# Two tiles of 25 taken from on-chip feature columns instead of gathered, in a graph layer

## The chip, the cores and the metric

One core of one Trainium2 chip. The time is that of one execution on the device, in microseconds, given as the median of several runs.

## What is computed

A layer of a graph network on N = 12500 nodes with 128 features and E = 400000 edges, sorted by destination. `h` is the normalised x, cut at zero. Each edge makes a message from the features of its two ends and 32 attributes of its own, the messages of a node are added up, and a gated unit makes the new features.

```python
h = jnp.maximum(_layernorm(x, axis=-1), 0.0)
hh = jnp.concatenate([h[src], h[dst], edge_attr_32], axis=-1)
m = jax.nn.relu(hh @ w1 + b1) @ w2 + b2
agg = jax.ops.segment_sum(m, dst, num_segments=12500)
gi = agg @ w_ih + b_ih
gh = h @ w_hh + b_hh
r = jax.nn.sigmoid(i_r + h_r)
z = jax.nn.sigmoid(i_z + h_z)
n = jnp.tanh(i_n + r * h_n)
return x + (1.0 - z) * n + z * h
```

## The kernel before, in words

A first stage (to about 85 us) normalises x, keeps `hT`, the features of all nodes as columns (128 partitions x 12544), in on-chip memory, and stores `p_rows`, the product of each node's features with the first third of w1, to DRAM.

The second stage goes over the edges in 125 chunks, each of five groups, each of five tiles of 128 edges. `step(c, s)` of every engine handles group s of chunk c; the order on each engine is written out by hand, with a lag of one to three steps between engines (`before`, `after`), and semaphores join them. Chunks 0 to 3 and the last are written out; the others are a hardware loop (`over_chunks`). Per group:

- GpSimd gathers the product rows of the edges' sources from `p_rows` into `rows`, one indirect DMA per tile (L488), as soon as the group's buffer is free (`seg_ready`).
- SyncE loads indices (L361), destinations (L378) and edge attributes (L381).
- VectorE makes the comparison table `lhs` (`build_lhs`, L902), adds the gathered rows to TensorE's product (`add_pre`, L934), and makes the table of ones that sorts messages to nodes (`build_onehot`, L893). `add_segments` (L937 to L946) adds the sums of a set of groups to `acc`; `candidate_pre`, `update` and `residual` (L952 to L972) finish the nodes of an earlier chunk. A set is groups 0 to 2 or 3 and 4.
- TensorE multiplies attributes, destination part and bias (`pre_activation`, L1174), sums the messages (`segment_sums`, L1194) and makes the gates (L1208 to L1212).
- ScalarE applies the relu (`relu_message`, L660), copies windows (L634, L640) and applies the gate functions.

One tile of the 25, the last of group 3, is not gathered. Its 128 source columns are copied one by one out of `hT` into `picked`, 96 by ScalarE and 32 by VectorE, 24 and 8 in each of steps 0 to 3, and TensorE multiplies them (L1179). Each engine first loads the node numbers of a step into registers (`load_picks`, L645 on ScalarE, L916 on VectorE), and each copy (L654, L925) then takes its column's address from a register:

```python
for e, node in enumerate(nodes, N_DVE + sum(PICKS_ACT[:s])):
    last = nc.scalar.copy(picked[:, e:e + 1], hT[:, bass.ds(node, 1)])
```

So GpSimd makes 24 gathers in a chunk. The node numbers come with two small loads of SyncE ahead of chunk 0 (L409).

Of the kernel before, what the change touches and what calls it, by code (L numbers as in the profile page):

```python
# [5 lines left out]
ALU = mybir.AluOpType  # L6
ACT = mybir.ActivationFunctionType
AX = mybir.AxisListType
F32 = mybir.dt.float32
I32 = mybir.dt.int32  # L10

P = 128
# [3 lines left out]
N = 12500  # L16
NT = -(-N // P)
NPAD = NT * P
# [12 lines left out]
T = 5  # L31
# [27 lines left out]
PGAP = P + 4  # L59
PICKED = 3  # L60
PICKS_DVE = (8, 8, 8, 8, 0)
PICKS_ACT = (24, 24, 24, 24, 0)
N_DVE, N_ACT = sum(PICKS_DVE), sum(PICKS_ACT)
assert N_DVE + N_ACT == P
IN_RANGE = "src holds node indices, 0 to N - 1"
BASE_IN_RANGE = "the window's base is a least node index, and a minimum holds it at BMAX"
# [6 lines left out]
def gather_tiles(s):  # L73
    return T - 1 if s == PICKED else T


def gnn_kernel(nc, x, src_cols, dst_cols, dst_rows, src_tiles, dst_tiles, ea_t, w1, b1, w2, b2, w_ih, b_ih, w_hh, b_hh, out):
# [3 lines left out]

    q_rows = nc.dram_tensor("q_rows", [NPAD, D], F32, kind="Internal").ap()
    sum_rows = nc.dram_tensor("sum_rows", [NPAD, ROW], F32, kind="Internal").ap()

    with ExitStack() as ctx:
        def sb(name, shape, dt=F32):
            return ctx.enter_context(nc.sbuf_tensor(name, shape, dt))
# [31 lines left out]

        base_i = low[ED:ED + 1, at:at + CHUNKS * NSETS].bitcast(I32)  # L120
        at += CHUNKS * NSETS
        assert at <= NPAD

        pick_dve = low[2 * ED:2 * ED + 1, 0:CHUNKS * N_DVE].bitcast(I32)
        pick_act = low[3 * ED:3 * ED + 1, 0:CHUNKS * N_ACT].bitcast(I32)
# [4 lines left out]
        onehot = sb("onehot", [P, 1 + max(ONEHOT_PLACE), T, WB])  # L130
        base_bc = sb("base_bc", [P, CHUNKS * NSETS])
        lhs = sb("lhs", [P, G, T, PGAP])
# [6 lines left out]
        w1_keep = sb("w1_keep", [P, D])  # L139
        picked = sb("picked", [P, P])  # L140
        idx = sb("idx", [P, G, T], I32)
# [98 lines left out]
        fin_chain = sem("fin_chain")  # L240
        pick_in, picked_dve, picked_act = (sem(n) for n in ("pick_in", "picked_dve", "picked_act"))

        g_zeroed, g_mask_set, g_scattered, g_chain, g_b1_in = (sem(n) for n in ("g_zeroed", "g_mask_set", "g_scattered", "g_chain", "g_b1_in"))
# [66 lines left out]
        def _(sp):  # L310
# [30 lines left out]
            sp.dma_start(dst_nat, dst_rows).then_inc(dstn_in, 16)  # L341
            sp.dma_start(w1_keep[:], w1[0:D, :]).then_inc(weights_in, 16)
            turns = BATCHES // 2 - LOADS_AHEAD
            with sp.Fori(0, turns - 1) as i:
# [49 lines left out]
            def fast():  # L394
                load_destinations(0)
                for s in range(AHEAD):
                    load_group(0, s)

                sp.wait_ge(acc_zeroed, 2)
                for par in range(2):  # L400
                    sp.wait_ge(p_stored[par], BATCHES // 2 * 16)
                    sp.wait_ge(hT_kept[par], BATCHES // 2)
                sp.dma_start(deg[0:1, 0:N], acc[0:1, 0:N]).then_inc(deg_zeroed, 16)
                sp.wait_ge(ranges_ready, 1)
                sp.wait_ge(w2ih_copied, 2)
                tile = PICKED * T + T - 1
                nodes = src_tiles.rearrange("(c k) p -> k c p", k=G * T)[tile:tile + 1, :, :]
                for row, first, last in ((pick_dve, 0, N_DVE), (pick_act, N_DVE, P)):
                    sp.dma_start(row.rearrange("o (c e) -> o c e", e=last - first), nodes[:, :, first:last]).then_inc(pick_in, 16)  # L409
                over_chunks(sp, chunk)  # L410
# [121 lines left out]
        def _(act):  # L532
# [109 lines left out]
            def load_picks(c, s):  # L642
                if isinstance(c, int) and c == 0:
                    act.wait_ge(pick_in, 32)
                _, nodes = nc.values_load_multi_w_load_instructions(  # L645
                    pick_act[0:1, bass.ds(c * N_ACT + sum(PICKS_ACT[:s]), PICKS_ACT[s])], (mybir.EngineType.Activation,),
                    min_val=0, max_val=N - 1, skip_runtime_bounds_check_because=IN_RANGE)
                return nodes

            def pick_columns(c, s, nodes):  # L650

                wait(act, pre_ready[PICKED], c)
                for e, node in enumerate(nodes, N_DVE + sum(PICKS_ACT[:s])):
                    last = nc.scalar.copy(picked[:, e:e + 1], hT[:, bass.ds(node, 1)])  # L654
                last.then_inc(picked_act, 1)

            def relu_message(c, s):
                act.wait_ge(summed[s], c + 1)
                m = rows[:, s, 0:gather_tiles(s), :]
                nc.scalar.activation(m, m, ACT.Relu).then_inc(message_ready[s], 1)  # L660
                if s == PICKED:

                    nc.scalar.activation(rows[:, s, T - 1, :], pre_ps[s % 2][:, (T - 1) * D:GE], ACT.Relu).then_inc(message_ready[s], 1)
# [22 lines left out]
            def step(c, s):  # L686
# [11 lines left out]
                if old:  # L698
                    relu_message(*old)
                if exists((c, s)) and PICKS_ACT[s]:  # L700
                    pick_columns(c, s, load_picks(c, s))
                if s == 0 and ending is not None:
# [68 lines left out]
        def _(dve):  # L771
# [141 lines left out]
            def load_picks(c, s):  # L913
                if isinstance(c, int) and c == 0:
                    dve.wait_ge(pick_in, 32)
                _, nodes = nc.values_load_multi_w_load_instructions(  # L916
                    pick_dve[0:1, bass.ds(c * N_DVE + sum(PICKS_DVE[:s]), PICKS_DVE[s])], (mybir.EngineType.DVE,),
                    min_val=0, max_val=N - 1, skip_runtime_bounds_check_because=IN_RANGE)
                return nodes

            def pick_columns(c, s, nodes):

                wait(dve, pre_ready[PICKED], c)
                for e, node in enumerate(nodes, sum(PICKS_DVE[:s])):
                    last = nc.vector.tensor_copy(picked[:, e:e + 1], hT[:, bass.ds(node, 1)])  # L925
                last.then_inc(picked_dve, 1)

# [46 lines left out]
            def step(c, s):  # L974
# [9 lines left out]
                if exists((c, s)):  # L984
                    build_lhs(c, s)
                    if s in ENDS:
                        sum_counts(c, ENDS[s])
                if s != 1 and old:
                    add_pre(*old)
                if old:  # L990
                    build_onehot(*old)
                if exists((c, s)) and PICKS_DVE[s]:
                    pick_columns(c, s, load_picks(c, s))
                if s == 1 and exists((c, s)):
# [36 lines left out]

            def fast():
                over_chunks(dve, chunk)
# [61 lines left out]
        def _(pe):  # L1095
# [64 lines left out]
            def pre_activation(c, s):  # L1160

                old = before(c, s, {0: 1, 1: 3}.get(s, 2))
                if old and old[1] == PICKED:

                    pe.wait_ge(message_ready[PICKED], old[0] * 2 + 2)
                elif old:
                    pe.wait_ge(summed[old[1]], old[0] + 1)
# [4 lines left out]
                for t in range(T):  # L1172
                    gathered = t < gather_tiles(s)
                    last = nc.tensor.matmul(pre_ps[s % 2][:, t * D:(t + 1) * D], lhs[:, s, t, 0:P],  # L1174
                                            rhs[:, k, :], start=True, stop=gathered)
                    if not gathered:
                        pe.wait_ge(picked_dve, (c + 1) * sum(n > 0 for n in PICKS_DVE))
                        pe.wait_ge(picked_act, (c + 1) * sum(n > 0 for n in PICKS_ACT))
                        last = nc.tensor.matmul(pre_ps[s % 2][:, t * D:(t + 1) * D], picked[:], w1_keep[:], start=False, stop=True)  # L1179
                last.then_inc(pre_ready[s], 1)  # L1180

            def segment_sums(c, s):

                k = SET_OF[s]
                pe.wait_ge(onehot_ready[s], c + 1)
                pe.wait_ge(message_ready[s], c * 2 + 2 if s == PICKED else c + 1)
                old = set_before(c, k)
# [168 lines left out]
```

## Time and profile before

| | us |
|---|---|
| median of 3 runs | 3851.58 |
| lowest, highest | 3850.6, 3860.34 |
| time of the profiled execution | 3857.86 |
| its span | 3856.0 |
| GpSimd, TensorE busy | 2861.7, 2920.9 |
| VectorE, ScalarE busy | 2076.1, 1921.0 |

The span is from the first to the last instruction. Busy time counts what an engine itself executes; register loads, register arithmetic and waits of its sequencer are not in it, and are seen only when a single source line is asked for. PE is TensorE, DVE VectorE, ACT ScalarE, POOL GpSimd, SP SyncE; a q behind the name is the engine's sequencer.

### The profile page before, as it was taken

Reading aid. Unit: us, or ns where it says so; the run is one execution under the profiler, and the core shown is the slowest. Engines: PE = TensorE matmul, PEld = TensorE weight load, DVE = VectorE, ACT = ScalarE, POOL = GpSimd, SP = SyncE. Lnnn points to the kernel's source line nnn. Section 1 sums busy time; section 2 is a strip of 40 time slices with the busy share of each in tenths; the row PEclk is TensorE's granted clock in tenths of the full one; section 3 lists DMA queues with packets and bytes.
Section 4 is the critical chain, followed back from the end, with each engine's and each line's share of the span. In section 5 each row is a group of like instructions: output and inputs, shape, how many; then the busy total and the mean of one; then the engine's idle time right before and its main releaser. Section 6 shows DMA issues by size and latency. Waiting matters only on the chain.

```text
span 3856.0 us, 94141 instructions
## 1 busy us (share of the span) xinstructions
PE 2920.9 (76%) x16157; PEld 2660.2 (69%) x16157; DVE 2076.1 (54%) x8517; ACT 1921.0 (50%) x13700; POOL 2861.7 (74%) x3039
## 2 busy tenths in 40 slices
PE   4677877777777778778777777777787787787777
PEld 4666767667667767667767776677676776677676
DVE  5555555555555555555555555555555555555554
ACT  5544555445554545445554455445554455545553
POOL 4677777777777777777777777777777777777775
PEclk8677677777777776776776677767767767767766
DMA  6444444444444444444444444444444444444443
GB/s 172 118 112 112 111 111 112 111 114 112 111 111 112 111 111 111 111 112 112 111 112 112 112 111 111 111 112 111 111 112 111 114 112 111 112 112 111 111 111 80
DMA packets 439213, 433.42 MB, mean 112 GB/s; under 512 B 180040, under 2 KB 331047, under 8 KB 439057
## 3 DMA queue, kind: packets, MB, share of 16 engines
q0 software_dynamic: 96000, 196.80, 23.5%
q1 hardware_dynamic: 314864, 223.36, 19.7%
q10 hardware_dynamic: 28318, 12.94, 1.2%
q14 instruction: 23, 0.19, 0.0%
q8 instruction: 8, 0.13, 0.0%
HBM read 419.89 MB, written 12.82 MB: 112 GB/s over the span
## 4 chain that ended last, share of the span: by engine, by line
POOL 51%; issue 23%; PE 14%; DMA 3%; ACT 3%; ACTq 2%; DVE 1%; POOLq 1%; DVEq 0%; SPq 0%
POOL rows L488 51%; PE ps L1194 6%; DMA rows<-p_rows,idx 3%; ACT picked L654 2%; ACTq L645 2%; PE ps L1174 2%; PE ps L1209 2%; PE ps L1211 1%; PE ps L1208 1%; DVE rows L934 1%; PE ps L1179 1%; PE ps L1212 1%; POOLq L257 0%; POOLq L285 0%; DVE low L946 0%
## 5 line engine op out<-in xcount | busy, mean ns | idle before, releaser
L488 POOL DMA_INDIRECT rows<-p_rows,idx x3000 | 2831.3, 944 | 938.5 <-issue 897.5
L654 ACT COPY picked<-hT 128x1 f32 x12000 | 1181.4, 187 | 552.9 <-issue 552.9
L1174 PE MATMUL ps<-rhs,lhs 128*128 128x128 f32 x6250 | 1113.4, 342 | 73.5 <-DVE rows L934 68.1
L1194 PE MATMUL ps<-onehot,rows 128*128 128x95 f32 x6250 | 1079.8, 338 | 112.5 <-DVE low L946 112.3
L1194 PEld LDWEIGHTS ps<-onehot,rows 128*128 128x128 f32 x6250 | 1039.0, 255 | 150.8 <-issue 150.8
L934 DVE TENSOR_TENSOR rows<-rows,ps 128x640 f32<-128x640 f32 x625 | 495.6, 793 | 1145.8 <-DMA rows<-p_rows,idx 1138.5
L1174 PEld LDWEIGHTS ps<-rhs,lhs 128*128 128x128 f32 x6250 | 1025.3, 252 | 105.2 <-DVE rows L934 71.5
L660 ACT ACTIVATE rows<-rows 128x640 f32<-128x640 f32 x625 | 447.0, 715 | 1214.0 <-DVE rows L934 1210.6
L902 DVE TENSOR_SCALAR_CACHE_REDUCE lhs<-dst_row,node_at 95x640 f32<-95x640 int32 x625 | 543.2, 869 | 5.3 <-DMA dst_row<-in_dst_rows_dram 5.3
L893 DVE TENSOR_TENSOR onehot<-dst_rel,ps 128x475 f32<-128x475 f32 x625 | 400.9, 642 | 0.0
L925 DVE COPY picked<-hT 128x1 f32 x4000 | 349.9, 146 | 8.0 <-DMA low<-in_src_tiles_dram 7.6
L945 DVE TENSOR_TENSOR acc<-acc,ps 128x95 f32 x250 | 63.5, 254 | 519.9 <-PE ps L1197 449.0
L1179 PE MATMUL ps<-w_keep,picked 128*128 128x128 f32 x250 | 72.6, 381 | 340.0 <-ACT picked L654 340.0
L1179 PEld LDWEIGHTS ps<-w_keep,picked 128*128 128x128 f32 x250 | 47.0, 236 | 361.9 <-issue 361.9
L1216 PE MATMUL ps<-ident,upd 128*100 128x128 f32 x123 | 43.7, 356 | 321.7 <-DVE upd L965 321.7
L1209 PE MATMUL ps<-low,b2ih 1*128 (+1 forms) x738 | 268.4, 464 | 0.0
L1216 PEld LDWEIGHTS ps<-ident,upd 128*100 128x100 f32 x123 | 16.9, 137 | 348.1 <-DVE upd L965 347.5
L1208 PE MATMUL ps<-acc,w2ih 128*128 (+1 forms) x738 | 225.9, 408 | 0.0
L1209 PEld LDWEIGHTS ps<-low,b2ih 1*128 1x128 f32 x738 | 178.4, 299 | 62.8 <-issue 59.6
L1208 PEld LDWEIGHTS ps<-acc,w2ih 128*128 128x128 f32 x738 | 192.2, 318 | 0.0
L1211 PE MATMUL ps<-hT,whh_sb 128*128 (+1 forms) x492 | 181.4, 472 | 0.0
L1158 PE MATMUL ps<-w_dst,h_win 128*95 128x128 f32 x500 | 115.7, 319 | 47.4 <-ACT h_win L634 47.4
(101 smaller groups left out, 1372.0 us busy)
## 6 DMA issues: line engine op xcount, KB each, us to landing
dst_row<-in_dst_rows_dram SPq DMA_DIRECT2D x625, 240.0 KB, 3.8
lhs<-in_ea_t_dram SPq DMA_DIRECT2D x625, 80.0 KB
rows<-p_rows,idx POOLq DMA_INDIRECT x3000
idx<-in_src_cols_dram SPq DMA_DIRECT2D x625, 2.5 KB
p_rows<-low SPq DMA_DIRECT2D x14, 448.0 KB, 3.2
x_fin<-in_x_dram ACTq DMA_DIRECT2D x123, 50.0 KB
out_dram<-out_fin ACTq DMA_DIRECT2D x123, 50.0 KB
acc<-in_x_dram SPq DMA_DIRECT2D x13, 448.0 KB, 4.8
```

The costliest lines, as they stand in the source:

```text
L488: pool.indirect_dma_start(out=rows[:, s, t, :], out_offset=None, in_=p_rows[:, :], in_offset=bass.IndirectOffsetOnAxis(ap=idx[:, s, t:t + ...
L654: last = nc.scalar.copy(picked[:, e:e + 1], hT[:, bass.ds(node, 1)])
L660: nc.scalar.activation(m, m, ACT.Relu).then_inc(message_ready[s], 1)
L893: nc.vector.tensor_tensor(onehot[:, ONEHOT_PLACE[s], :, 0:W], dst_rel[:, s * T:(s + 1) * T].unsqueeze(2).to_broadcast([P, T, W]), iota_ps. ...
L902: nc.vector.tensor_scalar(lhs[0:W, s, :, 0:P], dst_row[0:W, s, :].rearrange("w (t p) -> w t p", t=T), node_at[0:W, bass.ds(c * NSETS + SET ...
L925: last = nc.vector.tensor_copy(picked[:, e:e + 1], hT[:, bass.ds(node, 1)])
L934: nc.vector.tensor_tensor(r, r, pre_ps[s % 2][:, 0:k * D], ALU.add).then_inc(summed[s], 1)
L1174: last = nc.tensor.matmul(pre_ps[s % 2][:, t * D:(t + 1) * D], lhs[:, s, t, 0:P], rhs[:, k, :], start=True, stop=gathered)
L1194: done = nc.tensor.matmul(sg[:, 0:W], rows[:, s, t, :], onehot[:, ONEHOT_PLACE[s], t, 0:W], start=(first and t == 0), stop=(last and t == ...
L1208: nc.tensor.matmul(gate_ps[:, g, :], w2ih[:, cols], a, start=True, stop=False)
L1209: last = nc.tensor.matmul(gate_ps[:, g, :], b2ih[0:1, cols], d, start=False, stop=(g == 2))
L1211: nc.tensor.matmul(gate_ps[:, g, :], whh_sb[:, cols], h, start=False, stop=True)
```

## The change

Two tiles of the 25, the last of groups 3 and 4, are copied from `hT`; GpSimd makes 23 gathers a chunk. The 256 columns are shared as 120 to ScalarE (24 in each of five steps) and 136 to VectorE (32, 24, 24, 24, 32). ScalarE's copies see `picked` and `hT` as bytes and take four bytes from an address that is already in bytes: VectorE makes it once, as node x 4 + 66688, for all chunks, it goes to DRAM (`pick_dram`) and comes back in rows on one partition. VectorE's copies take f32 words by the node number as before. SyncE loads ten rows instead of two, ScalarE's five after the store of the made places. VectorE loads its registers ahead of `add_pre`, and copies the first half of its columns ahead of `build_onehot` and the second half behind it. TensorE waits for the relu of a copied tile only before its last tile.

```diff
-PICKED = 3
-PICKS_DVE = (8, 8, 8, 8, 0)
-PICKS_ACT = (24, 24, 24, 24, 0)
+PICKED = (3, 4)
+ACT_PICKS = ((0, 24), (56, 24), (104, 24), (152, 24), (200, 24))
+DVE_PICKS = ((24, 32), (80, 24), (128, 24), (176, 24), (224, 32))
...
+HT_AT = 66688
...
 def gather_tiles(s):
-    return T - 1 if s == PICKED else T
+    return T - 1 if s in PICKED else T
...
+                sp.wait_ge(places_ready, 1)
+                sp.dma_start(pick_dram, places).then_inc(places_stored, 16)
+                sp.wait_ge(places_stored, 16)
+                for k in range(G):
+                    first, n = ACT_PICKS[k]
+                    sp.dma_start(pick_act[k].rearrange("o (c e) -> o c e", e=n),
+                                 pick_dram.rearrange("(o c) e -> o c e", o=1)[:, :, first:first + n]).then_inc(pick_in, 16)
+                    first, n = DVE_PICKS[k]
+                    tile, e = PICKED[first // P] * T + T - 1, first % P
+                    sp.dma_start(pick_dve[k].rearrange("o (c e) -> o c e", e=n),
+                                 src_tiles.rearrange("(c k) p -> k c p", k=G * T)[tile:tile + 1, :, e:e + n]).then_inc(pick_in, 16)
...
-                for e, node in enumerate(nodes, N_DVE + sum(PICKS_ACT[:s])):
-                    last = nc.scalar.copy(picked[:, e:e + 1], hT[:, bass.ds(node, 1)])
+                for k in part:
+                    e = 4 * (first + k)
+                    last = nc.scalar.copy(picked_bytes[:, e:e + 4], hT_bytes[:, bass.ds(found[k] - HT_AT, 4)])
...
+            dve.wait_ge(src_in, 16)
+            nc.vector.tensor_scalar(places, places, 4, HT_AT, ALU.mult, ALU.add).then_inc(places_ready, 1)
...
+                    found = load_picks(c, s)
+                    half = DVE_PICKS[s][1] // 2
                 if s != 1 and old:
                     add_pre(*old)
+                if exists((c, s)):
+                    pick_columns(c, s, found, range(half))
                 if old:
                     build_onehot(*old)
-                if exists((c, s)) and PICKS_DVE[s]:
-                    pick_columns(c, s, load_picks(c, s))
+                if exists((c, s)):
+                    pick_columns(c, s, found, range(half, len(found)))
...
+                    if t == T - 1 and old and old[1] in PICKED:
+
+                        pe.wait_ge(message_ready[old[1]], old[0] * 2 + 2)
```

How it moves instructions. VectorE, step 3 of the loop's chunk, before (L902 is the comparison, L934 the addition, L893 the onehot, L916 the register load, L925 the copies, each with one register operation, listed as ISA):

```order
L902 TENSOR_SCALAR lhs,count<-dst_row,node_at 95x5x128
L934 TENSOR_TENSOR rows<-rows,ps 128x640 [waits rows_in1,pre_ready1]
L893 TENSOR_TENSOR onehot<-dst_rel,ps 128x5x95 [waits dst_rel_ready,seg_ready4]
L916 ISA
L916 TENSOR_LOAD low
L925 ISA [waits pre_ready3]
L925 COPY picked<-hT 128x1
```

The same step in the changed kernel (L935 is the comparison, L952 the load, L970 the addition, L960 the copies):

```order
L935 TENSOR_SCALAR lhs,count<-dst_row,node_at 95x5x128
L952 ISA [waits pre_ready4]
L952 TENSOR_LOAD low
L970 TENSOR_TENSOR rows<-rows,ps 128x640 [waits rows_in1,pre_ready1]
L960 ISA
L960 COPY picked<-hT 128x1
```

The load stands ahead of the addition; behind the addition come 12 pairs of ISA and COPY, then the onehot (L926), then 12 more pairs. The loop of VectorE has 128 rows before and 336 now.

ScalarE, step 3 of the loop's chunk, before (L660 is the relu, L645 the load, L654 the copies, each of the 24 with an ISA between):

```order
L660 ACTIVATE rows<-rows 128x640 [waits summed1]
L645 ISA
L645 TENSOR_LOAD low
L654 ISA [waits pre_ready3]
L654 COPY picked<-hT 128x1
```

And changed (L691 the relu, L675 the load, L684 the copies):

```order
L691 ACTIVATE rows<-rows 128x640 [waits summed1]
L675 ISA [waits pre_ready4]
L675 TENSOR_LOAD low
L684 COPY picked<-hT 128x4 x24
```

The register operations between the copies are gone, and step 4, which had no copies, has the same rows.

## Rows read from the trace of the kernel before

**Rows 1.** The page, part 1: engine, busy us, share of the span, instructions.

```profile
PE 2920.9 (76%) x16157; PEld 2660.2 (69%) x16157; DVE 2076.1 (54%) x8517; ACT 1921.0 (50%) x13700; POOL 2861.7 (74%) x3039
```

**Rows 2.** Lines of GpSimd, 200 to 3800 us: busy, mean ns, idle before.

```profile
L488 POOL DMA_INDIRECT rows<-p_rows,idx x2884 | 2721.6, 944 | 878.9 <-issue 864.3 <-PE ps L1194 14.6
```

**Rows 3.** Timeline of VectorE over one chunk: start, us, what [idle before].

```profile
2002.91 0.69 DVE L934 TENSOR_TENSOR rows<-rows,ps 128x512 f32<-128x512 f32 x1 [3.15 <-DMA rows<-p_rows,idx]
2003.52 0.64 DVE L893 TENSOR_TENSOR onehot<-dst_rel,ps 128x475 f32<-128x475 f32 x1
...
2008.02 0.25 DVE L945 TENSOR_TENSOR acc<-acc,ps 128x95 f32 x1 [3.18 <-PE ps L1197]
...
2008.79 0.82 DVE L934 TENSOR_TENSOR rows<-rows,ps 128x640 f32<-128x640 f32 x1 [0.36 <-DMA rows<-p_rows,idx]
...
2015.12 0.82 DVE L934 TENSOR_TENSOR rows<-rows,ps 128x640 f32<-128x640 f32 x1 [1.72 <-DMA rows<-p_rows,idx]
...
2018.84 0.88 DVE L902 TENSOR_SCALAR_CACHE_REDUCE lhs<-dst_row,node_at 95x640 f32<-95x640 int32 x1
...
2021.27 0.82 DVE L934 TENSOR_TENSOR rows<-rows,ps 128x640 f32<-128x640 f32 x1 [1.55 <-DMA rows<-p_rows,idx]
...
2027.66 0.82 DVE L934 TENSOR_TENSOR rows<-rows,ps 128x640 f32<-128x640 f32 x1 [2.86 <-DMA rows<-p_rows,idx]
```

**Rows 4.** Source line L925, 2010 to 2012 us: sequencer and engine, first and last start.

```profile
L925 DVEq FUSED_REGOPS  x8: 46/46/46, 2010.1 to 2010.9; - x8
L925 DVE COPY picked<-hT x8: 136/138/143, 2010.9 to 2011.3; 128x1 f32 x8
```

**Rows 5.** Timeline of VectorE in chunk 0.

```profile
108.10 0.95 DVE L925 COPY picked<-hT 128x1 f32 x8
```

**Rows 6.** Register loads by source line: ns min/median/max, first and last start.

```profile
L916 DVEq TENSOR_LOAD <-low x500: 598/620/837, 105.1 to 3819.2; - x167
L645 ACTq TENSOR_LOAD <-low x500: 1475/1661/1695, 105.1 to 3820.0; - x167
L937 DVEq TENSOR_LOAD <-low x250: 318/529/544, 124.9 to 3841.3; - x125
L628 ACTq TENSOR_LOAD <-low x250: 279/457/470, 93.2 to 3806.4; - x125
```

**Rows 7.** Timeline of ScalarE, step 1 of the same chunk.

```profile
2009.65 0.74 ACT L660 ACTIVATE rows<-rows 128x640 f32<-128x640 f32 x1 [0.80 <-DVE rows L934]
2011.53 2.32 ACT L654 COPY picked<-hT 128x1 f32 x24 [1.15 <-issue]
```

**Rows 8.** Busy us (and count) of one chunk: PE, PEld, DVE, ACT, POOL; then TensorE's picks.

```profile
1997.60:2027.50 29.90, 23.84 (x125) 21.57 (x125) 16.19 (x66) 14.94 (x109) 22.59 (x25) 0.68 0.46 112
...
2026.45 0.77 PE L1179 MATMUL ps<-w_keep,picked 128*128 128x128 f32 x2 [2.93 <-ACT picked L654]
```

**Rows 9.** Timeline around chunk 0: SyncE's small loads, the first picks, chunk 1.

```profile
98.17 1.50 SPq L409 DMA_DIRECT2D low<-in_src_tiles_dram  x2
...
106.05 0.85 DVE L925 COPY picked<-hT 128x1 f32 x7 [7.62 <-DMA low<-in_src_tiles_dram]
...
117.09 0.87 DVE L902 TENSOR_SCALAR_CACHE_REDUCE lhs<-dst_row,node_at 95x640 f32<-95x640 int32 x1
```

**Rows 10.** Timeline of VectorE behind the last chunk's steps.

```profile
3830.50 0.69 DVE L934 TENSOR_TENSOR rows<-rows,ps 128x512 f32<-128x512 f32 x1 [3.74 <-DMA rows<-p_rows,idx]
...
3836.71 0.82 DVE L934 TENSOR_TENSOR rows<-rows,ps 128x640 f32<-128x640 f32 x1 [4.96 <-DMA rows<-p_rows,idx]
```

**Rows 11.** DMA issues: KB each, median us from issue to landing.

```profile
base_bc<-base_f_dram ACTq DMA_DIRECT2D x1, 125.0 KB, 3.0
```

**Rows 12.** Timeline of GpSimd while VectorE copies.

```profile
2011.26 0.94 POOL L488 DMA_INDIRECT rows<-p_rows,idx  x1 [0.30 <-PE ps L1194]
```

**Rows 13.** The page, part 3: DMA queues of the instructions: packets, MB.

```profile
q14 instruction: 23, 0.19, 0.0%
q8 instruction: 8, 0.13, 0.0%
```

More of the change, by code:

```diff
@@ L10 @@
 I32 = mybir.dt.int32
+U8 = mybir.dt.uint8
 P = 128
@@ L59, with turns_of @@
 PGAP = P + 4
-PICKED = 3
-PICKS_DVE = (8, 8, 8, 8, 0)
-PICKS_ACT = (24, 24, 24, 24, 0)
-N_DVE, N_ACT = sum(PICKS_DVE), sum(PICKS_ACT)
-assert N_DVE + N_ACT == P
-IN_RANGE = "src holds node indices, 0 to N - 1"
+PICKED = (3, 4)
+ACT_PICKS = ((0, 24), (56, 24), (104, 24), (152, 24), (200, 24))
+DVE_PICKS = ((24, 32), (80, 24), (128, 24), (176, 24), (224, 32))
+assert sorted(e for first, n in ACT_PICKS + DVE_PICKS for e in range(first, first + n)) == list(range(len(PICKED) * P))
+def turns_of(picks, slot):
+    return max(k + 1 for k, (first, _) in enumerate(picks) if first < (slot + 1) * P)
+HT_AT = 66688
+IN_RANGE = "src holds node indices, 0 to N - 1, and they are made into places in a row of hT"
 BASE_IN_RANGE = "the window's base is a least node index, and a minimum holds it at BMAX"
@@ L118, in gnn_kernel, with pick_row @@
         at += 2 * NB * D
[L120 to L125, printed above, removed]
+        base_i = low[ED:ED + 1, NPAD - CHUNKS * NSETS:NPAD].bitcast(I32)
+        assert at <= NPAD - CHUNKS * NSETS
+        def pick_row(part, at, picks):
+            out = []
+            for _, n in picks:
+                out.append(low[part:part + 1, at:at + CHUNKS * n].bitcast(I32))
+                at += CHUNKS * n
+            assert at <= N
+            return out
+        pick_act = pick_row(ED, 0, ACT_PICKS[:4]) + pick_row(2 * ED, 0, ACT_PICKS[4:])
+        pick_dve = pick_row(2 * ED, CHUNKS * ACT_PICKS[4][1], DVE_PICKS[:2]) + pick_row(3 * ED, 0, DVE_PICKS[2:])
         dst_int = sb("dst_int", [P, G * T], I32)
@@ L130, in gnn_kernel @@
         onehot = sb("onehot", [P, 1 + max(ONEHOT_PLACE), T, WB])
+        places = onehot[:, :, :, :].rearrange("p g t w -> p (g t w)")[0:CHUNKS, 0:len(PICKED) * P].bitcast(I32)
         base_bc = sb("base_bc", [P, CHUNKS * NSETS])
@@ L241, in gnn_kernel @@
         pick_in, picked_dve, picked_act = (sem(n) for n in ("pick_in", "picked_dve", "picked_act"))
+        src_in, places_ready, places_stored = (sem(n) for n in ("src_in", "places_ready", "places_stored"))
         g_zeroed, g_mask_set, g_scattered, g_chain, g_b1_in = (sem(n) for n in ("g_zeroed", "g_mask_set", "g_scattered", "g_chain", "g_b1_in"))
@@ L342, in _ @@
             sp.dma_start(w1_keep[:], w1[0:D, :]).then_inc(weights_in, 16)
+            first, gap = PICKED[0] * T + T - 1, (PICKED[1] - PICKED[0]) * T
+            picked_tiles = src_tiles.rearrange("(c k) p -> c k p", k=G * T)[:, first:first + gap + 1:gap, :]
+            sp.dma_start(places.rearrange("c (k p) -> c k p", p=P), picked_tiles).then_inc(src_in, 16)
             turns = BATCHES // 2 - LOADS_AHEAD
@@ L405, in fast @@
                 sp.wait_ge(w2ih_copied, 2)
[L406 to L409, printed above, removed]
+                sp.wait_ge(places_ready, 1)
[9 more added lines that the diff above has]
+                                 src_tiles.rearrange("(c k) p -> k c p", k=G * T)[tile:tile + 1, :, e:e + n]).then_inc(pick_in, 16)
                 over_chunks(sp, chunk)
@@ L642, in load_picks, with pick_columns @@
             def load_picks(c, s):
[L643 to L652, printed above, removed]
-                for e, node in enumerate(nodes, N_DVE + sum(PICKS_ACT[:s])):
-                    last = nc.scalar.copy(picked[:, e:e + 1], hT[:, bass.ds(node, 1)])
-                last.then_inc(picked_act, 1)
+                if isinstance(c, int) and c == 0 and s == 0:
+                    act.wait_ge(pick_in, 32 * G)
+                first, n = ACT_PICKS[s]
+                wait(act, pre_ready[PICKED[first // P]], c)
+                _, found = nc.values_load_multi_w_load_instructions(
+                    pick_act[s][0:1, bass.ds(c * n, n)], (mybir.EngineType.Activation,),
+                    min_val=HT_AT, max_val=HT_AT + 4 * (N - 1), skip_runtime_bounds_check_because=IN_RANGE)
+                return found
+            def pick_columns(c, s, found, part):
+                first = ACT_PICKS[s][0]
+                for k in part:
+                    e = 4 * (first + k)
+                    last = nc.scalar.copy(picked_bytes[:, e:e + 4], hT_bytes[:, bass.ds(found[k] - HT_AT, 4)])
+                if part[-1] == len(found) - 1:
+                    last.then_inc(picked_act, 1)
             def relu_message(c, s):
@@ L699, in step @@
                     relu_message(*old)
-                if exists((c, s)) and PICKS_ACT[s]:
-                    pick_columns(c, s, load_picks(c, s))
+                if exists((c, s)):
+                    pick_columns(c, s, load_picks(c, s), range(ACT_PICKS[s][1]))
                 if s == 0 and ending is not None:
@@ L913, in load_picks, with pick_columns @@
             def load_picks(c, s):
[L914 to L917, printed above, removed]
-                    min_val=0, max_val=N - 1, skip_runtime_bounds_check_because=IN_RANGE)
[L919 to L926, printed above, removed]
+                if isinstance(c, int) and c == 0 and s == 0:
+                    dve.wait_ge(pick_in, 32 * G)
+                first, n = DVE_PICKS[s]
+                wait(dve, pre_ready[PICKED[first // P]], c)
+                _, found = nc.values_load_multi_w_load_instructions(
+                    pick_dve[s][0:1, bass.ds(c * n, n)], (mybir.EngineType.DVE,),
+                    min_val=0, max_val=N - 1, skip_runtime_bounds_check_because=IN_RANGE)
+                return found
+            def pick_columns(c, s, found, part):
+                first = DVE_PICKS[s][0]
+                for k in part:
+                    last = nc.vector.tensor_copy(picked[:, first + k:first + k + 1], hT[:, bass.ds(found[k], 1)])
+                if part[-1] == len(found) - 1:
+                    last.then_inc(picked_dve, 1)
             def add_pre(c, s):
@@ L1162, in pre_activation @@
                 old = before(c, s, {0: 1, 1: 3}.get(s, 2))
-                if old and old[1] == PICKED:
-                    pe.wait_ge(message_ready[PICKED], old[0] * 2 + 2)
-                elif old:
+                if old:
                     pe.wait_ge(summed[old[1]], old[0] + 1)
@@ L1176, in pre_activation @@
                     if not gathered:
-                        pe.wait_ge(picked_dve, (c + 1) * sum(n > 0 for n in PICKS_DVE))
-                        pe.wait_ge(picked_act, (c + 1) * sum(n > 0 for n in PICKS_ACT))
-                        last = nc.tensor.matmul(pre_ps[s % 2][:, t * D:(t + 1) * D], picked[:], w1_keep[:], start=False, stop=True)
+                        slot = PICKED.index(s)
+                        pe.wait_ge(picked_dve, c * G + turns_of(DVE_PICKS, slot))
+                        pe.wait_ge(picked_act, c * G + turns_of(ACT_PICKS, slot))
+                        last = nc.tensor.matmul(pre_ps[s % 2][:, t * D:(t + 1) * D], picked[:, slot * P:(slot + 1) * P], w1_keep[:],
+                                                start=False, stop=True)
                 last.then_inc(pre_ready[s], 1)
@@ L1185, in segment_sums @@
                 pe.wait_ge(onehot_ready[s], c + 1)
-                pe.wait_ge(message_ready[s], c * 2 + 2 if s == PICKED else c + 1)
+                pe.wait_ge(message_ready[s], c * 2 + 2 if s in PICKED else c + 1)
                 old = set_before(c, k)
```

9 lines of the change are left out of this document (6 added, 3 removed).

## The prediction

> **What bounds the kernel now.** I read the page's busy times first, then the grouped lines of GpSimd, then one chunk of VectorE in order of time, and last the single source lines, because only there do the instructions of an engine's sequencer (register loads and register arithmetic) show. The page gives no engine more than 76% [rows 1], so it names no bound. GpSimd does: between 200 and 3800 us its 2884 gathers take 944 ns each, and nearly all its idle time is "issue", 864 us, or 0.30 us per gather; only 14.6 us are waits for TensorE [rows 2]. So the gathers follow each other every 1.249 us, 24 of them make a chunk of 29.95 us, and 125 chunks make the kernel. Everything else waits for them: VectorE's addition stands idle until the rows have come in five of the six places of a chunk where it waits [rows 3].
>
> **What the change removes.** One gather per chunk: 23 x 1.249 = 28.7 us. If GpSimd still bounded, 125 x 1.249 = 156 us would go.
>
> **What it adds on VectorE.** The path that matters there is not the engine's but its sequencer's. In the chunk of rows 3, eight register operations of the picks run from 2010.1 to 2010.9, seven intervals, so 0.114 us each, while the eight copies that they feed, handed over in advance behind a longer operation, start within 2010.9 to 2011.3, 0.06 us apart [rows 4]. So a copied column costs the engine 0.06 us and the sequencer 0.114 us, and when nothing longer is in front the copies come out at the sequencer's pace: eight in 0.95 us, (0.95 - 0.15)/7 = 0.114 [rows 5]. VectorE now copies 136 columns per chunk instead of 32, still with a register operation each: 104 x 0.1145 = **11.9 us** more.
>
> Then the register loads. VectorE's load of eight node numbers takes 0.62 us in the median (0.60 to 0.84), its load of one value 0.53; ScalarE's load of 24 takes 1.66, its load of one 0.46 [rows 6]. From ScalarE a value costs (1.66 - 0.46)/23 = 0.052 us; from VectorE's own pair (0.62 - 0.53)/7 = 0.013, or 0.044 with the slower half of its loads (0.84). I take ScalarE's slope, because its load has the new size: 24 values 1.65 us, 32 values 2.08 us. Three and two of them make 9.1 us per chunk where four loads of eight, 0.6 and 0.82 in turn, made 2.85: **+6.3 us**, and 0.1 for issuing a fifth. With the low slope they would be 3 x 0.83 + 2 x 0.93 = 4.3 us, only 1.5 more; with 0.06 a value they would reach 10.5, 7.7 more. Those are the two ends.
>
> To what does this add? VectorE's sequencer waits only at its six marked places. Each wait is the idle time in brackets in rows 3 and, since the sequencer is through once it has handed out the instruction in front, the part in which that one still runs: 3.15 and 0.8 of a comparison, 4.0; 3.18 less a register load of 0.53, 2.6; 0.36 and 0.2, 0.6; 1.72 and 0.1, 1.8; 2018.84 to 2021.27, 2.4; 2.86 and 0.1, 3.0. That is 14.4, or 14.0 with the hand-over itself taken off, in a turn of 29.95, so its own work is about 16.0 us [rows 3], and the sum **16.0 + 11.9 + 6.3 + 0.1 = 34.3 us**. That is more than GpSimd's 28.7 and more than the 29.95 of now: 14 us of room are filled with 18.3 us of new work. The long operations do not add to it: an addition (0.82), a table of ones (0.64) or a comparison (0.87) runs while the sequencer loads registers or hands out the next twelve copies (1.37 us). The addition of group 4 is shorter by a tile (0.69 against 0.82), which is hidden too.
>
> **What waits for VectorE then.** In a step the register load now stands ahead of the addition, and half of the copies ahead of the onehot, as the rows of the program order show. Where VectorE has time, the load falls into the wait for the rows and costs nothing; in a chunk that VectorE bounds, there is no such wait, and the addition, the relu, the segment sums and the release of the row buffers all come later. GpSimd will then stand at its wait for the segment sums, about 34.3 - 28.7 = 5.6 us a chunk.
>
> **ScalarE.** It copies 120 columns instead of 96 and loses its register operations. Its 24 copies take 2.32 us, 0.093 each, and the idle time before them is 1.15 us of load behind a relu [rows 7]. I cost the removed register operation at nothing, since copies were already at the engine's pace as far as these rows tell (each lasts longer than the 0.093 us between two starts); four bytes instead of a word I cost between 0 and 0.09 us each. A step is 1.88 us from the relu's start to the first copy [rows 7] and 2.3 of copies; five of those, two window copies with their loads (0.9 each) and the gate functions (1.3) make about 24 us, 35 at the high end of the byte copies, where it would only draw level with VectorE. Fifth turn, one relu of a tile more (0.26 us): inside. TensorE has one product pair of picks more a chunk, 0.77 us on 23.8 [rows 8], with 10 us of room in a chunk of 34.3.
>
> **Start and end.** The first picks started at 106.05 us, 7.9 us after SyncE issued their two small loads at 98.17, 0.75 us each [rows 9]. Now SyncE first stores the made places (0.75 to issue, about 3.0 to land, the landing time of a small transfer of ScalarE's in the same phase [rows 11]), waits, and issues ten such loads, 7.5 us; with the same 6.4 us of landing the first copy comes near 98.2 + 3.7 + 7.5 + 6.4 = 115.8, **9.7 us later**. Making the places is one operation on 125 partitions in front of it, hidden in SyncE's earlier work. Chunk 0 had 11.0 us of VectorE from there (106.05 to the first comparison of chunk 1 at 117.09 [rows 9]) and gets 18.3 more: 29.3. Chunks 1 and 2 have no finishing work on VectorE (candidate, update, residual, 1.6 us): 32.7 each. 122 chunks at 34.3 are 4184.6. Behind the last one the old kernel needed 3856.0 - 3826.8 (3830.50 less 3.74 of waiting) = 29 us, with waits for the last gathers of 3.74 and 4.96 us in it [rows 10]; TensorE's work behind them stays, so I take off 5: 24. Sum: 115.8 + 29.3 + 65.4 + 4184.6 + 24 = **4419 us** of span. The profiled execution had a span of 3856.0 and a time of 3857.9, and the median of the three runs is 3851.6, 6.3 below it; so 4419 + 1.9 - 6.3 = 4415 as a median.
>
> Its own range: the period is good to about 1 us (overlap of the chained operations, the load of 32): 4290 to 4540; with the ends of the load cost 3830 and 4590.
>
> **Against a rule.** While VectorE's eight copies ran from 2010.9 to 2011.3 [rows 4], a gather began at 2011.26, 0.30 us behind the one before and 0.94 long, like all the others [rows 12]: copies cost GpSimd nothing. The Trainium skill, SBUF — State Buffer, "Who interferes with whom", says that VectorE copies can take the port pair shared with GpSimd and block its making of descriptors. By that rule 136 copies of 0.06 us could add 8.2 us to GpSimd's 28.7, a chunk of 36.9. The trace speaks against it at this shape.
>
> **Rivals.**
> - *GpSimd stays the bound, 3705 us, 8%.* The sequencer would have to hand out columns at the engine's 0.06 us: 34.3 - 136 x 0.0545 = 26.9, under 28.7. Then 3857.9 - 156 + 9.7 - 6.3 = 3705. For it: the engine can do it [rows 4]; against: the register operations never come closer than 0.114. The decision lies at 5.6 us per chunk, 0.073 us a column.
> - *Long register loads are cheap, about 3840 us, 6%.* With the low slope a chunk is 16.0 + 11.9 + 1.5 + 0.1 = 29.5, and gain and loss cancel: 115.8 + 24.5 + 55.8 + 3599 + 24 = 3819, up to 3840 with 0.2 us more a chunk. Against: ScalarE's 1.66 us.
> - *The longer loop has to be fetched in every turn, about 4780 us, 9%.* VectorE's loop grows from 128 to 336 rows of program. A transfer per turn of 3.0 us [rows 11] on top gives 122 x 3.0 = 366 more. Against: ScalarE's loop of 228 rows ran with 31 packets on the instruction queues in the whole run [rows 13], so it was fetched once. The Trainium skill, Runtime: NRT & Kernel Launch, "Instruction fetch mechanics", says that the buffer holds two blocks of 256 instructions and that a branch out of them stalls; by that rule it hangs on where the 336 lie.
> - *Copies do block GpSimd, about 4740 us, 2%*, with a chunk of 36.9.
> - *ScalarE bounds through slow byte copies, 4300 to 4600 us, 3%*: a slower outcome too, only with another engine in front.
>
> **How the numbers follow.** Forecast 72%; together nine in ten lie above the present time. Range: 4150 to 4800 leaves out the first two rivals (14%) and holds the fetch and port cases and the unknown costs between. A difference under 0.3%, some 12 us, counts as no change, and a measurement of this kernel can tell no less. Faster 0.10 (the first rival and a share of the second), same 0.02, slower 0.88.
>
> **What would show it.** Right: GpSimd's idle before its gathers put down to TensorE's sums, some 5 us a chunk; VectorE's wait for rows gone; VectorE loads of 1.6 and 2.1 us; register operations 0.114 apart; VectorE busy near 16.2 + 104 x 0.06 = 22 us of 34 [rows 8], so never "full" on the page. Wrong: gathers still every 1.25 us without waits (first rival), loads under 1 us (second), thousands of packets on the instruction queues (third), gathers longer than 0.95 us (fourth), or VectorE waiting for ScalarE's picks through TensorE (fifth).

## The result and the profile after

The changed kernel takes 4464.6 us in the median (4462.55 to 4465.33, four runs) against 3852.6 us of the kernel before: a ratio of 1.158, 95% interval 1.157 to 1.160, 612 us slower. The forecast was 4415 (4150 to 4800).

The page of the changed kernel, part 1 (engine, busy us, share of the span, instructions), answers to [rows 1]:

```profile
PE 2838.4 (64%) x16407; PEld 2634.7 (59%) x16407; DVE 3155.7 (71%) x21518; ACT 2212.8 (50%) x16825; POOL 2742.7 (61%) x2914
```

GpSimd fell from 74% to 61% busy; VectorE is the highest now, but at 71% it looks as if it had room. The longest wait of the changed kernel, and the waits of VectorE's addition and of GpSimd (total us, times, longest):

```profile
ACT rows L691 <- DVE rows L970: 1415.0, 621, 7.7
DVE rows L970 <- issue: 846.9, 499, 2.5
POOL rows L515 <- issue: 808.4, 2529, 1.1
POOL rows L515 <- PE ps L1238: 690.6, 201, 23.7
POOL rows L515 <- PE ps L1241: 141.2, 144, 2.3
```

In the kernel before, the same view has this line of VectorE's addition:

```profile
DVE rows L934 <- DMA rows<-p_rows,idx: 1138.5, 533, 5.0
```

Where the addition waited 1138 us for gathered rows, it now waits for no one that the profile shows ("issue"), ScalarE's relu waits 1415 us for the addition, and GpSimd waits 832 us for TensorE's segment sums, some 6.7 us in each of 125 chunks. On GpSimd's timeline this stands as two kinds of row; the gathers themselves are unchanged, 0.94 us with 0.30 between [rows 2, 12]:

```profile
2001.17 0.94 POOL L515 DMA_INDIRECT rows<-p_rows,idx  x1 [5.38 <-PE ps L1238]
2002.42 0.94 POOL L515 DMA_INDIRECT rows<-p_rows,idx  x1 [0.31 <-issue]
```

The period can be read off an operation that each chunk has once, VectorE's last addition of the finishing work (source line, 300 to 3600 us: count, ns, first and last start), in the kernel before and, in the second block, in the changed one:

```profile
L972 DVE TENSOR_TENSOR out_fin<-x_fin,ps x110: 286/287/290, 315.8 to 3581.8; 100x128 f32<-100x128 f32 x110
```

```profile
L1008 DVE TENSOR_TENSOR out_fin<-x_fin,ps x94: 286/289/290, 332.6 to 3566.0; 100x128 f32<-100x128 f32 x94
```

3266.0/109 = 29.96 us and 3233.4/93 = 34.77 us. The timeline of VectorE over two steps of one chunk (step 4, then step 0 of the next) answers to [rows 3]:

```profile
2002.99 0.15 DVE L944 TENSOR_REDUCE set_count<-count 95x1 f32<-95x2 f32 x1
2005.35 0.82 DVE L970 TENSOR_TENSOR rows<-rows,ps 128x640 f32<-128x640 f32 x1 [2.21 <-issue]
2006.09 1.25 DVE L960 COPY picked<-hT 128x1 f32 x16
2007.29 0.65 DVE L926 TENSOR_TENSOR onehot<-dst_rel,ps 128x475 f32<-128x475 f32 x1
2007.86 1.42 DVE L960 COPY picked<-hT 128x1 f32 x16
2009.85 0.88 DVE L935 TENSOR_SCALAR_CACHE_REDUCE lhs<-dst_row,node_at 95x640 f32<-95x640 int32 x1 [0.57 <-issue]
...
2012.42 0.69 DVE L970 TENSOR_TENSOR rows<-rows,ps 128x512 f32<-128x512 f32 x1 [1.69 <-issue]
```

The 2.21 us in front of the addition are the register load of 32 values. The source lines show it and the register operations, which no busy share contains; they answer to [rows 6] and [rows 4] (all loads of the run, then the five of one chunk, then the register operations):

```profile
L952 DVEq TENSOR_LOAD <-low x625: 1597/1827/2356, 108.5 to 4434.9; - x157
...
L952 DVEq TENSOR_LOAD <-low x1: 2111/2111/2111, 2003.1 to 2003.1; - x1
L952 DVEq TENSOR_LOAD <-low x1: 2218/2218/2218, 2010.0 to 2010.0; - x1
L952 DVEq TENSOR_LOAD <-low x1: 1829/1829/1829, 2017.7 to 2017.7; - x1
L952 DVEq TENSOR_LOAD <-low x1: 1608/1608/1608, 2024.7 to 2024.7; - x1
L952 DVEq TENSOR_LOAD <-low x1: 1819/1819/1819, 2031.5 to 2031.5; - x1
...
L960 DVEq FUSED_REGOPS  x17000: 46/46/53, 110.9 to 4441.1; - x198
```

9.6 us a chunk are register loads, in which VectorE's sequencer hands out nothing.

### The profile page after: what moved, and what is told of

Its sections match the earlier page's. It is cut to its first block and busy times, and to the rows that moved or that the text cites. A ratio compares the mean times of both kernels' runs of the same rounds, so it can differ in the third digit from the quotient of the medians.

```text
span 4463.5 us, 112268 instructions
## 1 busy us (share of the span) xinstructions
PE 2838.4 (64%) x16407; PEld 2634.7 (59%) x16407; DVE 3155.7 (71%) x21518; ACT 2212.8 (50%) x16825; POOL 2742.7 (61%) x2914
## 5 line engine op out<-in xcount | busy, mean ns | idle before, releaser
L515 POOL DMA_INDIRECT rows<-p_rows,idx x2875 | 2712.3, 943 | 1651.2 <-issue 808.4
L684 ACT COPY picked<-hT 128x4 uint8 x15000 | 1488.5, 189 | 599.4 <-issue 599.3
L960 DVE COPY picked<-hT 128x1 f32 x17000 | 1460.4, 148 | 101.4 <-issue 101.0
L1216 PE MATMUL ps<-rhs,lhs 128*128 128x128 f32 x6250 | 1192.0, 359 | 64.7 <-DVE rows L970 51.9
L1216 PEld LDWEIGHTS ps<-rhs,lhs 128*128 128x128 f32 x6250 | 1112.3, 270 | 85.8 <-issue 65.6
L691 ACT ACTIVATE rows<-rows 128x640 f32<-128x640 f32 x625 | 433.6, 694 | 1420.5 <-DVE rows L970 1415.0
L970 DVE TENSOR_TENSOR rows<-rows,ps 128x640 f32<-128x640 f32 x625 | 477.4, 764 | 847.7 <-issue 846.9
L935 DVE TENSOR_SCALAR_CACHE_REDUCE lhs<-dst_row,node_at 95x640 f32<-95x640 int32 x625 | 543.4, 869 | 79.2 <-issue 68.2
L926 DVE TENSOR_TENSOR onehot<-dst_rel,ps 128x475 f32<-128x475 f32 x625 | 406.0, 650 | 0.0
L1222 PE MATMUL ps<-w_keep,picked 128*128 128x128 f32 x500 | 129.2, 347 | 288.7 <-ACT picked L684 288.7
L1253 PE MATMUL ps<-low,b2ih 1*128 (+1 forms) x738 | 169.7, 309 | 0.0
L1252 PE MATMUL ps<-acc,w2ih 128*128 (+1 forms) x738 | 145.2, 278 | 0.8
L1253 PEld LDWEIGHTS ps<-low,b2ih 1*128 1x128 f32 x738 | 107.9, 183 | 35.9
L1255 PE MATMUL ps<-hT,whh_sb 128*128 (+1 forms) x492 | 114.4, 314 | 0.0
```

The source lines that it names most:

```text
L515: pool.indirect_dma_start(out=rows[:, s, t, :], out_offset=None, in_=p_rows[:, :], in_offset=bass.IndirectOffsetOnAxis(ap=idx[:, s, t:t + ...
L684: last = nc.scalar.copy(picked_bytes[:, e:e + 4], hT_bytes[:, bass.ds(found[k] - HT_AT, 4)])
L926: nc.vector.tensor_tensor(onehot[:, ONEHOT_PLACE[s], :, 0:W], dst_rel[:, s * T:(s + 1) * T].unsqueeze(2).to_broadcast([P, T, W]), iota_ps. ...
L935: nc.vector.tensor_scalar(lhs[0:W, s, :, 0:P], dst_row[0:W, s, :].rearrange("w (t p) -> w t p", t=T), node_at[0:W, bass.ds(c * NSETS + SET ...
L960: last = nc.vector.tensor_copy(picked[:, first + k:first + k + 1], hT[:, bass.ds(found[k], 1)])
L970: nc.vector.tensor_tensor(r, r, pre_ps[s % 2][:, 0:k * D], ALU.add).then_inc(summed[s], 1)
```

## The experiments

The theory: VectorE's sequencer sets the period, by a sum of copies with register operations, register loads and its old work. The rivals: waits for other engines behind the moved load and the later addition; the engine's own time; the loop being fetched anew. Periods below are from the same once-a-chunk operation as above.

**e1, bytes on both engines.** VectorE copies as ScalarE does, from ready addresses; SyncE loads its rows from `pick_dram` too.

```diff
...
-                    last = nc.vector.tensor_copy(picked[:, first + k:first + k + 1], hT[:, bass.ds(found[k], 1)])
+                    e = 4 * (first + k)
+                    last = nc.vector.tensor_copy(picked_bytes[:, e:e + 4], hT_bytes[:, bass.ds(found[k] - HT_AT, 4)])
```

> VectorE copies bytes from ready addresses too, so its 136 register operations a chunk are gone. Theory (VectorE's sequencer sets the period of 34.7 us): a copy then costs the sequencer only its hand-over, 0.114 - 0.046 = 0.068 us, so 136 x 0.046 = 6.3 us go and the period is 28.5, just under GpSimd's 23 x 1.249 = 28.7; some steps will still be late, so 28.7 to 29.3 a chunk and 3720 to 3800 us in all, faster than the kernel before. Rival (the engine or the load order sets it, or the lengthened loop is fetched in each turn): 34 us a chunk and over 4350 us.

Measured: 4086.4 us, ratio 1.060 (1.058 to 1.062), 31.77 us a chunk. The direction was right, the size was not: 3.0 us a chunk went instead of 6.3. VectorE's timeline of e1, a step with 24 copies:

```profile
2015.50 0.82 DVE L970 TENSOR_TENSOR rows<-rows,ps 128x640 f32<-128x640 f32 x1 [1.74 <-issue]
2016.24 0.94 DVE L960 COPY picked<-hT 128x4 uint8 x12
2017.09 0.64 DVE L925 TENSOR_TENSOR onehot<-dst_rel,ps 128x475 f32<-128x475 f32 x1
2017.65 0.94 DVE L960 COPY picked<-hT 128x4 uint8 x12
2018.50 0.25 DVE L997 TENSOR_TENSOR upd<-hT,cand 128x100 f32<-128x100 f32 x1
```

From the addition to the next operation there is no gap: 3.00 us, and the changed kernel takes 3.02 for the same stretch (2026.49 to 2029.51). With the register operations gone the sequencer is ahead and the engine itself is the bound there, and a copy of four bytes takes it (0.94 - 0.16)/11 = 0.071 us, more than the 0.06 of a word [rows 4]. I had let the engine's time vanish under the sequencer's. What e1 did gain came elsewhere: 1.0 and 1.1 us in the two steps with 32 copies (from addition to comparison 3.6 us in step 4, where the changed kernel takes 4.5, with 0.57 of it at the loop's branch), and 0.8 us in step 1, where the load and the copies stand behind the comparison.

**e2, a quarter of VectorE's copies left out.** The copy in front of each takes two neighbouring columns.

```diff
+                    if k % 4 == 1:
+                        continue
+                    w = 2 if k % 4 == 0 else 1
-                    last = nc.vector.tensor_copy(picked[:, first + k:first + k + 1], hT[:, bass.ds(found[k], 1)])
+                    last = nc.vector.tensor_copy(picked[:, first + k:first + k + w], hT[:, bass.ds(found[k], w)])
```

> Of VectorE's 136 copies a chunk every fourth is left out, and the one in front of it copies two neighbouring columns (so 34 columns hold another node's features). Register loads unchanged. Theory: 34 x 0.1145 = 3.9 us less a chunk, period 30.8 us, about 3985 us in all. Rival (the period is waits for other engines behind the later addition): less than 1 us a chunk, over 4340 us.

Measured: 4391.0 us, 34.31 us a chunk, only 0.45 less. By the expectation's own bounds this spoke for the rival. But the trace has a new wait, at the first operation behind the loop's branch (timeline; then the total of these waits), and the instruction queue has 622 packets where [rows 13] has 23:

```profile
2003.97 0.96 DVE L963 COPY picked<-hT 128x2 f32 x12
2008.00 0.87 DVE L935 TENSOR_SCALAR_CACHE_REDUCE lhs<-dst_row,node_at 95x640 f32<-95x640 int32 x1 [3.07 <-issue]
...
DVE lhs L935 <- issue: 374.4, 121, 3.5
...
q14 instruction: 622, 5.10, 0.4%
```

3.07 us once a turn, against 68.2 us in 121 such waits (0.56) in the changed kernel. That is the sign of the prediction's third rival, met in another kernel: e7 and e8 below test it.

**e3, short register loads in two steps.** Loads of 32 values become loads of 8, each used four times.

```diff
-                    pick_dve[s][0:1, bass.ds(c * n, n)], (mybir.EngineType.DVE,),
+                    pick_dve[s][0:1, bass.ds(c * n, 8 if n == 32 else n)], (mybir.EngineType.DVE,),
...
-                return found
+                return list(found) * 4 if n == 32 else found
```

> VectorE's two register loads of 32 values a chunk load 8 values, and each value is used four times (wrong columns in those two steps). Copies unchanged. Theory: the loads of 2.11 to 2.22 us become 0.6 to 0.8, so 2.7 to 3.0 us a chunk go, period 31.8 to 32.0, about 4110 us. Rival (loads lie beside other work and only copies count): no change, 4460 us.

Measured: 3787.9 us, below the kernel before, and 29.34 us a chunk: 5.4 us less instead of 2.8. The source lines of e3 tell why (load, then copies, then register operations):

```profile
L952 DVEq TENSOR_LOAD <-low x625: 597/1609/1845, 108.8 to 3761.0; - x157
...
L960 DVE COPY picked<-hT x17000: 132/144/156, 109.7 to 3765.0; 128x1 f32 x198
L960 DVEq FUSED_REGOPS  x11000: 46/46/53, 109.7 to 3762.9; - x197
```

The copies are still 17000, but the register operations fell from 17000 to 11000: since each value is used four times, its address is computed once. So the edit took away two things, about 3.1 us of loads (2 x (2.16 - 0.60)) and 48 register operations a chunk; the other 2.3 us are 0.048 us for each of those, the 46 ns that the rows show. The run prices both terms together, and it shows that neither the gathers nor TensorE hold the period at 34.8.

**e4, ScalarE back to words with register operations.**

```diff
...
-                    e = 4 * (first + k)
-                    last = nc.scalar.copy(picked_bytes[:, e:e + 4], hT_bytes[:, bass.ds(found[k] - HT_AT, 4)])
+                    last = nc.scalar.copy(picked[:, first + k:first + k + 1], hT[:, bass.ds(found[k], 1)])
```

> ScalarE's part of the change is undone: it copies f32 words with a register operation in front of each, by node numbers. Theory: ScalarE's copies go back from 0.095 to 0.093 us, its chunk stays near 24 us, and the time stays within 10 us of the changed kernel's 4465. Rival (the ready addresses matter for the period through TensorE's wait for the picks): some us a chunk longer, 4600 us or more.

Measured: 4470.0 us, 5 above the changed kernel, 34.77 a chunk. ScalarE's copies by ready addresses bring nothing and cost nothing here.

**e5 and e6, another split.** 40 of VectorE's 136 columns go to ScalarE; e5 with bytes on both engines, e6 with the changed kernel's words on VectorE. The on-chip rows that hold the numbers of the picked nodes are laid out to match.

```diff
-ACT_PICKS = ((0, 24), (56, 24), (104, 24), (152, 24), (200, 24))
-DVE_PICKS = ((24, 32), (80, 24), (128, 24), (176, 24), (224, 32))
+ACT_PICKS = ((0, 32), (48, 32), (96, 32), (152, 32), (200, 32))
+DVE_PICKS = ((32, 16), (80, 16), (128, 24), (184, 16), (232, 24))
...
```

> Bytes from ready addresses on both engines (as in e1), and 40 of VectorE's 136 columns moved to ScalarE: 96 and 160. Each engine still makes one register load a step. Theory (VectorE's own work sets the period, ScalarE has room): VectorE's 31.66 us a chunk of e1 less 40 x (0.073 + 0.052) = 26.7; ScalarE's own work, 34.7 less 12.9 us of waits, 21.9, plus 40 x (0.095 + 0.05) = 27.7; both under GpSimd's 28.7, so GpSimd bounds again: 3700 to 3760 us, 2 to 4% faster than the kernel before. Rival (the copies of a late engine still hold TensorE at the second picked tile): 29.9 us a chunk and no gain.

> The changed kernel with the split 96 and 160, VectorE still with f32 words and register operations. Theory: 34.73 - 40 x (0.1145 + 0.052) = 28.1 us of VectorE's own work a chunk, under GpSimd's 28.7: 3710 to 3790 us, within 1% of e5, so that the bytes matter little once the split is right. Rival (the register operations themselves are what costs): 30 us a chunk or more, over 3880 us.

Measured: e5 3709.0 us, ratio 0.963 (0.962 to 0.965); e6 3710.1 us, 0.963 (0.962 to 0.964). Both beat both kernels, and they are the same within their spread. The line of GpSimd's gathers in e6, 200 to 3600 us, and e6's once-a-chunk operation:

```profile
L515 POOL DMA_INDIRECT rows<-p_rows,idx x2722 | 2570.4, 944 | 829.5 <-issue 777.4 <-PE ps L1238 29.6 <-PE ps L1241 22.5
```

```profile
L1008 DVE TENSOR_TENSOR out_fin<-x_fin,ps x115: 279/285/290, 321.0 to 3597.4; 100x128 f32<-100x128 f32 x115
```

3276.4/114 = 28.74 us a chunk: GpSimd is back at its pace of 23 x 1.249, and 52 us of waits for TensorE in 3400 are left (74 in the whole run, where the changed kernel has 832). This is the gain that the first rival of the prediction named (3705 us), reached by giving VectorE less to do.

**e7 and e8, the place of the loop.** Tiny writes of VectorE ahead of the chunks, 40 in front of e2's loop, 170 in front of the changed kernel's.

```diff
+                for k in range(170):
+                    t = out_fin[:, k:k + 1] if k < D else upd[:, k - D:k - D + 1]
+                    nc.vector.memset(t, 0.0)
                 over_chunks(dve, chunk)
```

> e2 with 40 tiny writes of VectorE in front of the chunks, which move the place of its loop in the program by 40 instructions and do nothing else. e2 had 622 packets on the instruction queue and 3.07 us of VectorE waiting at the top of every turn. Theory (the loop lay over one instruction block too many, and 40 instructions further it does not): the packets fall to about 25, the 3.07 us go, 31.2 us a chunk, about 4015 us. Rival (the wait at the top of the loop has another cause): 4390 us as in e2.

> The changed kernel with 170 tiny writes in front of VectorE's chunks, nothing else changed. If the place of the loop in the program decides whether it is fetched anew, then 170 instructions should move the changed kernel's loop into the bad place: hundreds of packets on the instruction queue, some 3 us more a turn, about 4830 us. If only the length of the loop counted: 4475 us (10 us for the writes).

Measured: e7 3989.5 us, 30.97 us a chunk; e8 4886.9 us, 38.33 a chunk. The instruction queue of e7:

```profile
q14 instruction: 27, 0.22, 0.0%
```

and that of e8, with its waits at the loop's top and the timeline at the branch:

```profile
q14 instruction: 627, 5.13, 0.3%
...
DVE lhs L935 <- issue: 400.5, 121, 3.9
...
2030.66 1.77 DVE L960 COPY picked<-hT 128x1 f32 x16
2036.01 0.88 DVE L935 TENSOR_SCALAR_CACHE_REDUCE lhs<-dst_row,node_at 95x640 f32<-95x640 int32 x1 [3.58 <-issue]
```

The 170 writes themselves take 5 us once (99.8 to 104.9) and move the first copy by 0.5 us; the run is 422 us longer. 597 packets more in 120 turns are five a turn, 41 KB of program. The Trainium skill, Runtime: NRT & Kernel Launch, "Instruction fetch mechanics", says that the buffer holds two blocks of 256 instructions and that a branch to a block outside stalls. The four runs can be made to agree with it. A loop within two blocks stays in the buffer, one that reaches into a third does not. The loop of the changed kernel and of e8 has 336 rows, that of e2 and e7 268 (68 fewer, and as many fewer in each of the four chunks written out ahead of it). Against the changed kernel's loop, which is not fetched anew, e2's begins 272 rows earlier (it is fetched), e7's 232 earlier (it is not) and e8's 170 later (it is). With blocks of 256 all four come out if the changed kernel's loop begins about 7 to 15 rows behind the start of a block; where it does begin was not looked up. So that a block is 256 no run measures by itself; that the place decides, e2 with e7 and the changed kernel with e8 show.

With the fetch taken out, e2's question is answered too: 34.77 - 30.97 = 3.80 us for 34 copies, 0.112 us each. The theory had 0.1145.

**e9 and e10, the old order.** Register load and all copies stand behind the onehot, in the changed kernel (e9) and in e6 (e10).

```diff
-                    found = load_picks(c, s)
-                    half = DVE_PICKS[s][1] // 2
                 if s != 1 and old:
                     add_pre(*old)
-                if exists((c, s)):
-                    pick_columns(c, s, found, range(half))
                 if old:
                     build_onehot(*old)
                 if exists((c, s)):
-                    pick_columns(c, s, found, range(half, len(found)))
+                    found = load_picks(c, s)
+                    pick_columns(c, s, found, range(len(found)))
```

> The changed kernel with VectorE's order of before: register load and all copies behind the onehot, nothing else changed. Theory (the sequencer's own work sets the period, and its order does not change the sum): 34.7 us a chunk, 4465 us, within 20. Rival (the load in front of the addition is what delays the relu, the sums and so the chunk): 1 us a chunk or more faster, under 4340 us.

> e6 (words, split 96 and 160) with the same old order. There VectorE has 28.1 us of work in a turn of 28.7 and GpSimd bounds. If the order of the change is worth something, it is here, where the load can fall into the wait for the rows: then up to 1 us a chunk slower than e6, 3710 to 3830 us. If the room of 0.6 us is all that counts: 3710 us, within 10.

Measured: e9 4462.2 us, 34.72 a chunk; e10 3707.5 us (ratio 0.962, 0.961 to 0.964) against 3710.1 of e6. The order is worth nothing in either, within what these runs can tell. That TensorE now waits for the relu of a copied tile only before its last tile was not undone in any run.

## Why the prediction was right, point by point

- **The bound after.** "16.0 + 11.9 + 6.3 + 0.1 = 34.3 us" on VectorE's sequencer; measured 34.77. Copies: 0.112 us each by e7, against 0.1145 in the sum. Register loads: this is the term that was too small, 9.6 us in the chunk shown against 9.1, because the slope of ScalarE's loads gave 1.65 and 2.08 where VectorE's took 1.61 to 1.83 and 2.11 to 2.22. With 9.6 - 2.85 = 6.8 the sum is 34.8. Over 122 chunks the half microsecond is 57 us, more than the whole miss of 50. This is the one term found mis-sized; with it the sum meets the period, though the 16.0 us of VectorE's old work was not measured by itself.
- **Start and end.** The first copy came at 111.0 us, not 115.8. SyncE stored the places at 93.69, 4.5 us earlier than the 98.17 of [rows 9] that the forecast starts from; why it was early is not shown. Until the first of the ten loads (99.23) it took 5.5 us and not 3.7. The last load was issued by 106.6, and ScalarE and VectorE began to load registers at 108.5, so the first copy came 4.4 us behind the last issue and not 6.4. Chunk 0 took 26.8 us of VectorE (111.0 to 137.8) and not 29.3. The end took 22 us (copies done at 4441.4, span 4463.5) and not 24. Together some 9 us less than forecast, the other side of the loads' 57.
- **GpSimd's wait.** Forecast 5.6 us a chunk at TensorE's sums, measured 6.7 over all chunks. In 345 of these waits 0.30 us would have passed anyway between two gathers; without that it is 5.8.
- **VectorE never full on the page.** Forecast some 22 us of 34, measured 25 of 35 (71% of the span). The copies are the engine's largest group, 1460 us, and 1460/17000 = 0.086 us of busy time each: where they come out 0.114 apart, a copy of 0.146 us keeps the engine busy all the while, which the forecast's 0.06 left out. The 9.6 us of loads a chunk stand nowhere in it.
- **ScalarE at nothing.** e4 bears it out: 24 copies take 2.38 us, 0.095 each, with bytes, and the time moves by 5 us.
- **The moved load and the order.** I had said that they change nothing where VectorE bounds; e9 bears it out, and e10 adds that they change nothing where GpSimd bounds with so little room.
- **The first rival** was wrong for this kernel, but its 3705 us is where e5 and e6 arrive. **The second** (cheap long loads) fell with the rows of the loads. **The fetch** did not take place in the changed kernel (30 packets), by luck of its place: e8 is the same kernel 170 instructions further, at 4887 us, where the rival had forecast 4780; 50 us of the difference are the forecast's own miss, and most of the rest is that a stall took 3.6 us a turn and not 3.0. **The port rival** did not come either: with 17000 copies of VectorE the gathers stay at 943 ns in the mean, and at 944 with the four-byte copies of e1. The Trainium skill, SBUF — State Buffer, "Who interferes with whom", says that copies can take the shared ports in the modes that use two ports. Whether copies as narrow as these enter such a mode no run here shows, so the runs say only that these do not slow the gathers.
- What was not foreseen: the size of e1 and of e3. In both, the edit let the sequencer run ahead or took away more than it named, and the sum over one path went over to the other (e1) or lost a second term (e3).

## What to carry to other kernels

Work made of many tiny instructions can be paid by an engine's sequencer rather than by the engine: price it as hand-over with register operation, plus register load (here 0.112 us and 0.05 us a column), add it to what the sequencer does already, and compare that sum with the bound of the loop before any busy share. Keep the engine's own path as a second sum: in e1 it took over as soon as the first fell. When work is moved off the bounding engine, divide it by the room that each receiver has in its own sum; the same change was 16% slower with 136 columns on VectorE and 3.7% faster with 96. Look at the instruction queue's packets after every change that lengthens or moves a loop: in e2 and e8 5.1 MB there, where the other runs have 0.2 to 0.3, went with a wait of 3.1 to 3.6 us at the top of every turn, and in e2 it hid what the experiment measured.

## What the runs showed of the hardware that was not expected

- Where a long hardware loop lies in the program is worth up to 3.6 us a turn: 4887 against 4465 us for the same loop, 3990 against 4391 us for that of e2.
- A copy of four bytes in one column takes VectorE 0.071 us, one of a 32-bit word 0.06; on ScalarE 0.095 against 0.093.
- A register load grows with its values: on VectorE 0.53 us for one, 0.60 to 0.84 for 8, 1.61 to 1.83 for 24, 2.1 to 2.2 for 32 in the rows above, with two levels for the same count. What decides between the two levels was not tried.
